# A four-layer block kernel on one core: weights of an integer feed-forward rounded by another engine, and its matrix products issued in another order

## The chip, the core and the metric

The kernel runs on one core of one Trainium2 chip. The time is in device microseconds (us) of one execution; lower is better. The engines are PE (TensorE; PEld is its weight load), DVE (VectorE), ACT (ScalarE), POOL (GpSimd) and SP (SyncE, which here only issues DMAs). Each works through its own instructions in their order and waits for others by semaphores.

## What is computed

x has 32 rows of 128 tokens by 256 features: 4096 tokens in 32 tiles of 128. Four layers follow each other, each an attention-like block and a feed-forward block, both on a layer norm and with a residual. The change touches layer 1 alone:

```python
x = x + _L1_xcond_ref(_layernorm(x, axis=-1), ctx_1024, ctx_1024, condB_tau[:, None], fside_BxS2_0, ...)
x = x + _L1_ffn_ref(_layernorm(x, axis=-1), L1_ffn_w_gate, L1_ffn_w_up, L1_ffn_w_down)

def _weight_quant(w):
    scale = 1.0 / jnp.clip(jnp.mean(jnp.abs(w)), 1e-05)
    return jnp.clip(jnp.round(w * scale), -1.0, 1.0) / scale
def _act_quant(x):
    scale = 127.0 / jnp.clip(jnp.max(jnp.abs(x), axis=-1, keepdims=True), 1e-05)
    return jnp.clip(jnp.round(x * scale), -128.0, 127.0) / scale
```

The feed-forward has three weights of 256 by 1024 (gate, up, down). Each is made of the integers -1, 0 and 1 times one scale, and the activations ahead of every product are rounded to integers with a scale per token: y = down(silu(gate(x)) * up(x)).

## The kernel before, in words

The layers are stages, each with its own blocks of instructions for the engines, one behind the other: a stage starts when all engines have ended the one before. X, the residual stream of all tiles, and MV, its row means and variances, stay in SBUF throughout.

**The attention of layer 1** (`attention`, L152) runs over 8 groups `g` of 4 tiles `u`; t = 4g + u. In tile t PE issues the output rows of tile t-2 (`output_rows`, L472), the scores of tile t+1, four turns of the probabilities (`turn_probs`, L447), and the weighting by values (`weighted_values`, L461 and L464), whose start waits for DVE's division of the tile before. Between these, except in the last group, it puts the work for the next group into the bank `ps_m`: keys in the first tile of the group, x columns in the second, queries in the third, values in the fourth. ACT (`group` from L282 on) follows in that order: the copy of the output rows (`outputs`, L280), `exps` (L273) with PE's turns, what was put into `ps_m`, and in the first tile of a group four norms of the next group's tiles (L249). DVE (L592 on) issues per tile the division of tile t-1 (`divide`, L579 and L583), the softmax of tile t+1 (L568, L573), and the row statistics of tile t-2 (`row_stats`, L136 and L138), which wait for X. POOL (`group` from L364 on) adds the rows of tile t-2 to X (`rows`, L358 and L362).

**The weights** (`BitWeights`, L632). Their loads are issued at the attention's start. In group 5 ACT sums their absolute values, one weight per tile (`magnitudes`, L664). In tile 28 PE adds these over the partitions (`totals`, L670, into `ps_m`) and DVE makes the scales from them (`scales`, L676 and L679); PE waits for that (`mean_link`) in tile 29 before it writes `ps_m` again. In tiles 29, 30 and 31 POOL rounds one weight each (`rounded`, L681), behind the rows of that tile: three passes over 128x2048 numbers, each waiting for the one before:

```python
pool.tensor_scalar(r, r, self.wscale[:, n:n + 1], ROUND, ALU.mult, ALU.add)
pool.tensor_scalar(r, r, ROUND, 1.0, ALU.subtract, ALU.min)
pool.tensor_scalar(self.wb[self.names[n]][:, :], r, -1.0, None, ALU.max)
```

ROUND is 12582912.0: what is added to it is rounded to an integer. The rows of tiles 30 and 31 come last.

**The feed-forward** (`bit_ffn`, L1318) runs over the 32 tiles. For a tile, ACT makes the norm (L1372) into one of two buffers `xn`. DVE finds the largest magnitude, makes the factor and rounds (L1479, L1483, L1486). PE turns the rows into columns (L1426). ACT takes them out as bf16 into `xqT` (L1377), which has one buffer. PE multiplies with gate and up (`gates_and_ups`, L1436) into four banks, two each; it claims each bank when ACT or DVE has emptied it. ACT applies silu to the gates (L1384), and DVE multiplies by the ups into h (L1528) and finds h's largest magnitude (L1479) and its factor (L1483). ACT rounds h (`h_rounded`, L1389), PE turns it (`h_columns`, L1446), ACT takes the columns out (L1395), and PE multiplies with down (`sums`, L1454). DVE adds the result to X and makes the row statistics (`finish`, L1511 to L1517). The order in which each engine takes the tiles is written out by hand:

```python
# ACT, tile t
gates(t + 1); h_rounded(t); norm(t + 3); h_columns(t); x_columns(t + 2)
# PE, tile t
gates_and_ups(t + 1); h_columns(t); x_columns(t + 2); sums(t)
```

DVE's tile t is h(t), the maximum of x of tile t+2, the maximum of h(t), the factors, the rounding of x of tile t+2, the dequantizing factors, and `finish(t-1)`.

## Time and profile before

| | |
|---|---|
| median of 3 runs (lowest, highest) | 3458.16 us (3453.02, 3458.41) |
| the profiled execution's own time | 3459.26 us |
| its span | 3457.5 us |
| mean granted TensorE clock over the span | 0.959 of full speed |
| PE busy | 3138.2 us (91%) |
| DVE busy | 2359.8 us (68%) |
| ACT busy | 1109.2 us (32%) |
| POOL busy | 983.6 us (28%) |
| layer 1's attention | 892.0 to 1246.5 us of the span |
| layer 1's feed-forward | 1246.5 to 1436.6 us of the span |

The shares are means over all stages with different limits and say little about the two that the change touches; those are read by their own stretches and timelines. A timeline row has the start in us from the span's start, the duration, the engine, the line, the operation with its tiles and shapes, and how many of the same kind are merged; in brackets stands how long the engine was idle before it and whose work ended that. The duration of a merged row runs from its first start to its last end. Durations of instructions that follow each other on one engine can overlap a little, so spacings are taken from starts.

### The profile page before, as it was taken

The page shows a single profiled execution, that of the slowest core. Times are in us where ns is not written, and L with a number is a line of the kernel's source. Part 1 is how long each engine was busy: PE and PEld are TensorE (multiplying, and loading weights), DVE is VectorE, ACT ScalarE, POOL GpSimd, SP SyncE. Part 2 cuts the span into 40 slices and gives each one's busy share as a digit, 9 for nine tenths or more (in the row PEclk, how much of TensorE's full clock was granted, in tenths as well). Part 3 has the DMA queues.
Part 4 walks back from the last instruction along what each step waited for, and adds up shares of the span by engine and source line. Part 5 has one row for each costly group of instructions (what it writes and reads, how often), then busy time and mean ns, then how long its engine had stood idle before and what let it go on. Part 6 is the DMA issues. An engine that isn't in the chain of part 4 may idle for free. (4 is left out here: it accounts for less than half of the span.)

```text
span 3457.5 us, 67521 instructions
## 1 busy us (share of the span) xinstructions
PE 3138.2 (91%) x27670; PEld 2384.3 (69%) x27670; DVE 2359.8 (68%) x6222; ACT 1109.2 (32%) x1989; POOL 983.6 (28%) x1010
## 2 busy tenths in 40 slices
PE   5999999899599947777899999999999987999999
PEld 4776766566377724466688888888888875777444
DVE  5777355100477758654788888888888883778666
ACT  3444211122245548643322222222222212454100
POOL 2342000233234440000244344354354352342000
PEclk9999999999799979988899999999999998999999
DMA  3100220243410000112000000000000002100000
GB/s 125 39 26 2 71 70 19 58 117 81 127 35 30 2 10 1 55 49 92 31 1 2 1 1 2 1 1 2 1 2 1 1 1 76 38 26 2 13 19 19
DMA packets 81169, 108.24 MB, mean 31 GB/s; under 512 B 11744, under 2 KB 62176, under 8 KB 80480
## 3 DMA queue, kind: packets, MB, share of 16 engines
q1 hardware_dynamic: 74720, 95.40, 8.5%
q0 software_dynamic: 6144, 8.52, 1.3%
q8 instruction: 222, 3.64, 0.4%
q14 instruction: 83, 0.68, 0.1%
HBM read 87.00 MB, written 16.91 MB: 30 GB/s over the span
## 5 line engine op out<-in xcount | busy, mean ns | idle before, releaser
L2069 POOL TENSOR_TENSOR pk_hisig<-pk_hihot,pk_sigs 128x512 f16<-128x512 f16 x512 | 520.4, 1044 | 668.3 <-DVE pk_hihot L2276 667.4
L2130 PE MATMUL pk_ps<-pk_nt,ew_downT 128*128 128x128 f32 x4096 | 515.5, 279 | 0.0
L2130 PEld LDWEIGHTS pk_ps<-pk_nt,ew_downT 128*128 128x128 f32 x4096 | 479.7, 192 | 15.3 <-issue 15.3
L2171 PE MATMUL pk_ps<-ew_up,pk_act_h 128*128 128x256 f32 x2048 | 450.4, 381 | 0.9 <-DVE pk_act_h L2264 0.9
L2171 PEld LDWEIGHTS pk_ps<-ew_up,pk_act_h 128*128 128x128 f32 x2048 | 388.8, 191 | 53.1 <-issue 1.0
L2077 ACT ACTIVATE pk_act_h<-pk_ps 128x512 f32<-128x512 f32 x256 | 152.9, 597 | 542.2 <-PE pk_ps L2130 542.2
L2277 DVE TENSOR_TENSOR pk_lohot<-pk_iota_h,pk_ps 128x1024 f16<-128x1024 f16 x256 | 310.6, 1213 | 0.0
L579 DVE RECIPROCAL a_rden<-a_ps_o 128x256 f32<-128x256 f32 x96 | 168.3, 1753 | 159.4 <-PE a_ps_o L464 159.4
L568 DVE TENSOR_REDUCE a_mx<-a_ps_s 128x8 f32<-128x1024 f32 x192 | 226.0, 1219 | 54.8 <-PE a_ps_s L438 54.5
L273 ACT ACTIVATE a_pT<-a_ps_t 128x512 f32<-128x512 f32 x384 | 208.9, 599 | 144.2 <-PE a_ps_t L447 144.0
L2450 PE MATMUL mo_ps<-mw_we,mo_xnT 128*128 128x512 f32 x512 | 225.6, 599 | 0.0
L573 DVE TENSOR_TENSOR a_probs<-a_ps_s,a_mx 128x1024 f32<-128x1024 f32 x192 | 225.2, 1214 | 0.0
L447 PE MATMUL a_ps_t<-ident,a_probs 128*128 128x128 f32 x1536 | 209.5, 279 | 4.1 <-ACT a_pT L273 4.1
L2264 DVE TENSOR_TENSOR pk_act_h<-pk_act_h,pk_ps 128x512 f32<-128x512 f32 x256 | 174.8, 683 | 43.4 <-PE pk_ps L2158 40.2
L447 PEld LDWEIGHTS a_ps_t<-ident,a_probs 128*128 128x128 f32 x1536 | 171.2, 142 | 47.4 <-issue 28.9
L362 POOL TENSOR_TENSOR X<-a_y,a_tmp 128x256 f32<-128x256 f32 x96 | 69.8, 727 | 468.9 <-ACT a_y L280 467.2
L2158 PE MATMUL pk_ps<-pk_hisig,pk_lohot 128*128 128x64 f16 x4096 | 163.8, 194 | 23.8 <-DVE pk_act_h L2264 14.4
L2450 PEld LDWEIGHTS mo_ps<-mw_we,mo_xnT 128*128 128x128 f32 x512 | 97.2, 192 | 116.9 <-issue 116.9
L2158 PEld LDWEIGHTS pk_ps<-pk_hisig,pk_lohot 128*128 128x128 f16 x4096 | 154.7, 99 | 30.2 <-DVE pk_act_h L2264 18.5
L461 PE MATMUL a_ps_o<-a_pT,a_v 128*32 128x128 f32 x3072 | 159.6, 280 | 6.8 <-DVE a_oT L583 6.8
L2276 DVE TENSOR_TENSOR pk_hihot<-pk_iota_h,pk_ps 128x256 f16<-128x256 f16 x256 | 105.1, 411 | 79.3 <-ACT pk_sigs L2097 79.3
L1301 DVE TENSOR_TENSOR ro_tmp<-ro_ps,ro_b 128x256 f32<-128x256 f32 x32 | 13.6, 424 | 212.0 <-PE ro_ps L1272 212.0
(353 smaller groups left out, 5395.4 us busy)
## 6 DMA issues: line engine op xcount, KB each, us to landing
ro_w<-in_L_W SPq DMA_DIRECT2D x16, 1024.0 KB, 7.1
a_ctx_t<-in_ctxT SPq DMA_DIRECT2D x24, 512.0 KB, 3.8
a_tau<-in_tau SPq DMA_DIRECT2D x24, 256.0 KB, 4.1
a_delta<-in_delta SPq DMA_DIRECT2D x24, 256.0 KB, 4.4
X<-in_x SPq DMA_DIRECT2D x4, 1024.0 KB, 9.4
row_dram<-sh_row SPq DMA_DIRECT2D x8, 512.0 KB, 3.0
sum_dram<-sh_new SPq DMA_DIRECT2D x8, 512.0 KB, 2.9
X<-sum_dram SPq DMA_DIRECT2D x4, 1024.0 KB, 9.5
```

The lines of the kernel that those rows point to most:

```text
L273: act.activation(pT[:, 4 * j:4 * j + 4, :], ps_t[j % 2][:, :].rearrange("p (h n) -> p h n", h=4), ACT.Exp).then_inc(t_taken, 1)
L447: ins = pe.transpose(ps_t[j % 2][:, c * P:(c + 1) * P], probs[:, parity, j, c, :], ident[:, :])
L568: dve.tensor_reduce(maxima[n], halves[n], AX_X, ALU.max).then_inc(max_ready, 1)
L573: dve.tensor_tensor(probs[:, parity, 2 * n:2 * n + 2, :, :].rearrange("p c r n -> p r c n"), halves[n], mx[:, 8 * n:8 * n + 8].rearrange(" ...
L579: dve.reciprocal(rden[:, :], ps_o[:, D:2 * D]).then_inc(den_ready, 1)
L2069: ins = pool.tensor_tensor(hisig[:, buf, n, :, :, :], hi, sig2.broadcast_to([P, TP, 2, ECH]), ALU.mult)
L2130: ins = pe.matmul(hid.bank(f"h{c}")[:, j * P:(j + 1) * P], downT[:, k, e * P:(e + 1) * P], nt[:, s, k, :], start=(k == 0), stop=(k == KC - 1))
L2158: ins = pe.matmul(wts.bank(f"w{b}")[:, j * 2 * ECH:(j + 1) * 2 * ECH], lohot[:, buf, j, :], hisig[:, buf, n, j, :, :].rearrange("p r c -> ...
L2171: ins = pe.matmul(tail.bank("y")[:, 0:D], act_h[:, s, c, :], up[:, c, :], start=(c == 0), stop=(c == ECH - 1))
L2264: wts.take(dve.tensor_tensor(hv, hv, wts.bank(f"w{b}")[:, :].rearrange("p (j c) -> p c j", c=ECH), ALU.mult), f"w{b}")
L2277: ins = dve.tensor_tensor(lohot[:, buf, :, :], *against(0, P))
L2450: ins = pe.matmul(main.bank(f"e{q}_{u}")[:, :], xnT[:, s, k, u * P:(u + 1) * P], we[:, k, 2 * q:2 * q + 2, :].rearrange("p e n -> p (e n)" ...
```

## The change

Four things, all in layer 1:

- The absolute sums move from group 5 to group 3, and totals and scales from tile 28 to tile 17 (`TOTALS_AT`). PE now issues the totals ahead of that tile's turns and waits for the scales behind two of them; DVE makes the scales ahead of the softmax.
- POOL no longer rounds. ACT does, in 24 pieces of 128x512, two at the end of each of the tiles 18 to 29: for each weight four pieces with scale and ROUND, then four that subtract ROUND and write bf16. DVE limits each weight to -1 and 1 in one pass over 128x2048 bf16, at the end of its tiles 23, 27 and 31, and PE waits for the three (`clipped`) at the start of the feed-forward.
- In the feed-forward `xqT` has two buffers. PE takes `gates_and_ups` two tiles ahead and puts it between `h_columns(t)` and `sums(t)`; `x_columns`, three ahead, comes last.
- ACT takes the x columns out ahead of the norm instead of behind the h columns.

```diff
@@ -307,8 +307,11 @@
                         queries(g + 1, 1 - s, 1, m)
                     if more and u == 3:
                         values(g + 1, 1 - s, 1, m)
-                    if integers and g == GROUPS - 3 and u < 3:
+                    if integers and g == 3 and u < 3:
                         integers.magnitudes(act, u)
+                    if integers and 0 <= t - ROUND_FROM < 12:
+                        integers.rounded(act, 2 * (t - ROUND_FROM))
+                        integers.rounded(act, 2 * (t - ROUND_FROM) + 1)
...
@@ -372,8 +375,6 @@
                         keys(g + 1, 1 - s, 0)
                         split(g + 1, 1 - s)
                         keys(g + 1, 1 - s, 1)
-                    if integers and not more and u > 0:
...
@@ -496,15 +497,18 @@
                             pe.wait_ge(xt_taken, g * 2 + 4)
                         else:
                             pe.wait_ge(q_taken, g * KC + 2 * KC)
-                        if integers and not more and u == 1:
-                            pe.wait_ge(integers.mean_link, 1)
                         output_rows(t - 2, u % 2)
                     if u < G - 1:
                         scores(g, s, u + 1)
                     elif more:
                         scores(g + 1, 1 - s, 0)
+                    if integers and t == TOTALS_AT:
+                        m_after_y(t)
+                        integers.totals(pe, ps_m[:, D:D + 3])
                     turn_probs(t, u % 2, 0)
                     turn_probs(t, u % 2, 1)
+                    if integers and t == TOTALS_AT:
+                        pe.wait_ge(integers.mean_link, 1)
                     if more:
...
-                    if integers and not more and u == 0:
-                        m_after_y(t)
-                        integers.totals(pe, ps_m[:, D:D + 3])
...
@@ -594,12 +595,14 @@
                     t = g * G + u
                     if not at_start(t, 1):
                         divide(t - 1, (u + 1) % 2)
+                    if integers and t == TOTALS_AT:
+                        integers.scales(dve, ps_m[:, D:D + 3])
                     if not (is_last(g) and u == G - 1):
                         softmax(t + 1, (u + 1) % 2)
                     if not at_start(t, 2):
                         row_stats(t - 2)
-                    if integers and is_last(g) and u == 0:
-                        integers.scales(dve, ps_m[:, D:D + 3])
+                    if integers and t >= ROUND_FROM + 5 and (t - ROUND_FROM - 5) % 4 == 0:
+                        integers.limited(dve, (t - ROUND_FROM - 5) // 4)
...
 INNER = 1024
 ROUND = 12582912.0
+TOTALS_AT = 4 * G + 1
+ROUND_FROM = TOTALS_AT + 1
...
+        self.shift = sb("shift", [P, 2])
...
-        self.mean_link, self.scales_ready, self.round_link = (
-            keep["semaphore"]("bq_mean_link"), keep["semaphore"]("bq_scales_ready"), keep["semaphore"]("bq_round_link"))
+        self.mean_link, self.scales_ready = keep["semaphore"]("bq_mean_link"), keep["semaphore"]("bq_scales_ready")
+        self.shifted, self.whole, self.clipped = (
+            keep["semaphore"]("bq_shifted"), keep["semaphore"]("bq_whole"), keep["semaphore"]("bq_clipped"))
...
     def constants(self, pool):
         pool.memset(self.ones[:, :], 1.0).then_inc(self.consts, 1)
         pool.memset(self.wmean[:, :], 0.0).then_inc(self.consts, 1)
+        pool.memset(self.shift[:, 0:1], ROUND).then_inc(self.consts, 1)
+        pool.memset(self.shift[:, 1:2], -ROUND).then_inc(self.consts, 1)
...
-    def rounded(self, pool, n):
-        r, at = self.raw[n][:, :], 3 * n
-        pool.wait_ge(self.scales_ready, 1)
-        pool.tensor_scalar(r, r, self.wscale[:, n:n + 1], ROUND, ALU.mult, ALU.add).then_inc(self.round_link, 1)
-        pool.wait_ge(self.round_link, at + 1)
-        pool.tensor_scalar(r, r, ROUND, 1.0, ALU.subtract, ALU.min).then_inc(self.round_link, 1)
-        pool.wait_ge(self.round_link, at + 2)
-        pool.tensor_scalar(self.wb[self.names[n]][:, :], r, -1.0, None, ALU.max).then_inc(self.round_link, 1)
+    def rounded(self, act, i):
+        n, q = i // 8, i % 4
+        at = slice(q * 512, (q + 1) * 512)
+        r = self.raw[n][:, at]
+        if i % 8 < 4:
+            act.wait_ge(self.scales_ready, 1)
+            act.activation(r, r, ACT.Identity, scale=self.wscale[:, n:n + 1], bias=self.shift[:, 0:1]).then_inc(
+                self.shifted, 1)
+        else:
+            act.wait_ge(self.shifted, 4 * n + q + 1)
+            act.activation(self.wb[self.names[n]][:, at], r, ACT.Identity, bias=self.shift[:, 1:2]).then_inc(
+                self.whole, 1)
+
+    def limited(self, dve, n):
+        dve.wait_ge(self.whole, 4 * n + 4)
+        b = self.wb[self.names[n]][:, :]
+        dve.tensor_scalar(b, b, 1.0, -1.0, ALU.min, ALU.max).then_inc(self.clipped, 1)
...
-        shift = sb("shift", [P, 2])
+        shift = integers.shift
...
-        xqT = sb("xqT", [P, KC, P], BF16)
+        xqT = sb("xqT", [P, 2, KC, P], BF16)
...
-        @block.gpsimd
-        def _(pool):
-            pool.memset(shift[:, 0:1], ROUND).then_inc(consts, 1)
-            pool.memset(shift[:, 1:2], -ROUND).then_inc(consts, 1)
...
             def x_columns(t):
                 xt.wait_full(act, t, "xt")
-                xt.take(act.activation(xqT[:, :, :], xt.bank("xt")[:, 0:D].rearrange("p (k n) -> p k n", k=KC),
+                xt.take(act.activation(xqT[:, t % 2, :, :], xt.bank("xt")[:, 0:D].rearrange("p (k n) -> p k n", k=KC),
                                        ACT.Identity, bias=shift[:, 1:2]), "xt")
...
-            act.wait_ge(consts, 2)
...
@@ -1408,11 +1420,11 @@
                 if t + 1 < TILES:
                     gates(t + 1)
                 h_rounded(t)
+                if t + 2 < TILES:
+                    x_columns(t + 2)
                 if t + 3 < TILES:
                     norm(t + 3)
                 h_columns(t)
-                if t + 2 < TILES:
-                    x_columns(t + 2)
...
                         gu.claim(pe, t, f"{a}{n}")
                         for k in range(KC):
-                            ins = pe.matmul(gu.bank(f"{a}{n}")[:, :], xqT[:, k, :], wt[:, k, n * 512:(n + 1) * 512],
+                            ins = pe.matmul(gu.bank(f"{a}{n}")[:, :], xqT[:, t % 2, k, :], wt[:, k, n * 512:(n + 1) * 512],
...
-            x_columns(0)
-            gates_and_ups(0)
-            x_columns(1)
+            pe.wait_ge(integers.clipped, 3)
+            for t in range(2):
+                x_columns(t)
+                gates_and_ups(t)
+            x_columns(2)
             for t in range(TILES):
-                if t + 1 < TILES:
-                    gates_and_ups(t + 1)
                 h_columns(t)
                 if t + 2 < TILES:
-                    x_columns(t + 2)
+                    gates_and_ups(t + 2)
                 sums(t)
+                if t + 3 < TILES:
+                    x_columns(t + 3)
```

## Rows read from the trace of the kernel before

**Rows 1.** By stretch: busy us (instructions) of PE, PEld, DVE, ACT, POOL; granted clock; DMA; GB/s.

```profile
1207.00:1246.50 39.50, 10.17 (x91) 7.17 (x89) 6.92 (x13) 3.34 (x8) 37.90 (x16) 0.63 0.00 0
...
1260.00:1420.00 160.00, 119.04 (x742) 71.42 (x742) 133.93 (x311) 128.02 (x200) 0.00 (x0) 0.99 0.00 1
```

**Rows 2.** Timeline of the attention's end; start, duration, engine, line, and idle time before.

```profile
1205.01 2.34 DVE L573 TENSOR_TENSOR a_probs<-a_ps_s,a_mx 128x1024 f32<-128x1024 f32 x2
...
1211.93 0.43 DVE L136 BATCH_NORM_STATS2 a_bst<-X 128x6 f32<-128x256 f32 x1 [4.58 <-POOL X L362]
...
1212.49 1.73 DVE L579 RECIPROCAL a_rden<-a_ps_o 128x256 f32<-128x256 f32 x1
...
1214.80 0.65 PE L461 MATMUL a_ps_o<-a_pT,a_v 128*32 128x128 f32 x8 [4.98 <-DVE a_oT L583]
...
1244.81 0.72 POOL L362 TENSOR_TENSOR X<-a_y,a_tmp 128x256 f32<-128x256 f32 x1
...
1246.49 1.28 ACT L1398 ACT_TABLE_LOAD   x1 [13.05 <-PEq L154]
```

**Rows 3.** Timeline, PE in tile 30: first weighting, and the output rows behind the last.

```profile
1204.47 0.42 PE L461 MATMUL a_ps_o<-a_pT,a_v 128*32 128x128 f32 x8
...
1206.35 1.13 PE L472 MATMUL a_ps_m<-a_wo,a_oT 128*128 128x256 f32 x4
```

**Rows 4.** Timeline, ACT: behind a group's four norms, and at the end of a queries tile.

```profile
1047.39 1.09 ACT L273 ACTIVATE a_pT<-a_ps_t 128x512 f32<-128x512 f32 x2 [0.96 <-PE a_ps_t L447]
...
1063.38 0.39 ACT L280 ACTIVATE a_y<-a_ps_m 128x256 f32<-128x256 f32 x1 [1.22 <-PE a_ps_m L472]
1065.19 1.08 ACT L273 ACTIVATE a_pT<-a_ps_t 128x512 f32<-128x512 f32 x2 [1.42 <-PE a_ps_t L447]
```

**Rows 5.** Timeline of one steady tile of the feed-forward, in order of start.

```profile
1331.68 1.27 ACT L1384 ACTIVATE bf_gt<-bf_ps,bf_dq 128x512 f32<-128x512 f32 x2 [0.83 <-PE bf_ps L1436]
...
1332.83 1.24 ACT L1389 ACTIVATE bf_hr<-bf_h,bf_shift,bf_asc 128x1024 f32<-128x1024 f32 x1
1333.96 0.59 ACT L1372 ACTIVATE bf_xn<-X,bf_nmr,bf_rstd 128x256 f32<-128x256 f32 x1
...
1334.12 1.09 PE L1446 MATMUL bf_ps<-ident,bf_hr 128*128 128x128 f32 x8 [1.25 <-ACT bf_hr L1389]
1334.66 0.42 DVE L1479 TENSOR_REDUCE bf_amx<-bf_xn 128x1 f32<-128x256 f32 x1 [0.71 <-ACT bf_xn L1372]
1334.82 1.27 ACT L1395 ACTIVATE bf_hqT<-bf_ps,bf_shift 128x512 bf16<-128x512 f32 x2 [0.26 <-PE bf_ps L1446]
...
1335.65 1.10 PE L1454 MATMUL bf_ps<-bq_down,bf_hqT 128*128 128x256 bf16 x8 [0.21 <-ACT bf_hqT L1395]
1335.97 0.47 ACT L1377 ACTIVATE bf_xqT<-bf_ps,bf_shift 128x256 bf16<-128x256 f32 x1
...
1336.44 0.17 DVE L1483 RECIPROCAL bf_asc<-bf_amx 128x2 f32<-128x2 f32 x1
...
1336.59 1.03 PE L1436 MATMUL bf_ps<-bq_gate,bf_xqT 128*128 128x512 bf16 x4
...
1336.98 0.48 DVE L1511 SCALAR_TENSOR_TENSOR X<-bf_ps,bf_dq,X 128x256 f32<-128x256 f32 x1
...
1337.28 1.27 ACT L1384 ACTIVATE bf_gt<-bf_ps,bf_dq 128x512 f32<-128x512 f32 x2 [0.83 <-PE bf_ps L1436]
1337.45 1.03 PE L1436 MATMUL bf_ps<-bq_up,bf_xqT 128*128 128x512 bf16 x4
...
1338.14 1.41 DVE L1528 SCALAR_TENSOR_TENSOR bf_h<-bf_ps,bf_dq,bf_gt 128x512 f32<-128x512 f32 x2
```

**Rows 6.** Groups by line and shape: the nearest rows for the new passes.

```profile
L1389 ACT ACTIVATE bf_hr<-bf_h,bf_shift,bf_asc 128x1024 f32<-128x1024 f32 x28 | 34.6, 1237 | 0.0
...
L1806 DVE TENSOR_SCALAR wa_low<-wa_inside 128x512 f32<-128x512 f32 x8 | 3.4, 427 | 0.3
...
L1086 DVE TENSOR_TENSOR sh_lohot<-sh_iota_b,sh_lo 128x2048 bf16<-128x2048 bf16 x16 | 35.9, 2287 | 7.3 <-PE sh_ps L906 7.0
```

More of the change, by code:

```diff
@@ L374, in group @@
                         keys(g + 1, 1 - s, 1)
-                    if integers and not more and u > 0:
-                        integers.rounded(pool, u - 1)
             if integers:
@@ L667, in totals @@
     def totals(self, pe, dst):
-        pe.wait_ge(self.consts, 2)
+        pe.wait_ge(self.consts, 4)
         pe.wait_ge(self.sums_ready, 3)
@@ L673, in scales @@
     def scales(self, dve, src):
-        dve.wait_ge(self.consts, 2)
+        dve.wait_ge(self.consts, 4)
         dve.wait_ge(self.summed, 1)
@@ L1353, in bit_ffn @@
         ys = Ring(f"{tag}_ys", sem, banks[7:8], ["y"])
-        consts, rstd_sq, setup = sem("consts"), sem("rstd_sq"), sem("setup")
+        rstd_sq, setup = sem("rstd_sq"), sem("setup")
         nmr_ready = sem("nmr_ready")
```

## The prediction

> **What bounds the kernel now.** The change touches two neighbouring stages, so I read the table of stretches for them first, then the timeline at their border, then the timeline of one steady tile. In the table the attention's end is a hole: from 1207.0 to 1246.5 us PE works 10.17 us and DVE 6.92 us, while POOL is busy 37.90 of 39.5 us [rows 1]. The timeline says what POOL does there. The last softmax is through at 1205.01 + 2.34 = 1207.35 us, but the next row statistics on DVE start only at 1211.93, after 4.58 us of waiting for an X that POOL adds, and behind them in DVE's order stands the division that PE needs for its last tile: PE resumes at 1214.80 [rows 2]. POOL is late because each weight's three rounding passes stand between two tiles' rows. This happens twice more, and the stage ends at 1246.49. POOL's rounding is thus the end of the attention's critical path.
>
> The feed-forward has no busy engine at its limit: in 160 us PE has 119.04, DVE 133.93, ACT 128.02 [rows 1]. One tile takes 5.60 us: ACT's `gates` starts at 1331.68 and again at 1337.28 [rows 5]. The order on ACT is the ring that sets it: gates, `h_rounded`, norm, h columns, x columns, and then 0.83 us of waiting, because PE can multiply the next gates only once those x columns exist. Another 0.26 us goes before the h columns, for PE's transposes. DVE waits 0.71 us for the norm, once per tile [rows 5]; the rest of its tile, 5.60 - 0.71 = 4.89 us, is work and its own hand-offs.
>
> **The attention's end, part by part.** *Rounding leaves POOL.* Without it X of the late tiles is there early, and DVE's order alone counts. From the softmax's end at 1207.35: row statistics and division up to PE's last weighting take 1214.80 - 1211.93 = 2.87 us, so PE starts at 1210.25. That weighting takes 1206.35 - 1204.47 = 1.88 us at the upper clock [rows 3]; 1212.15. Division to PE took 1214.80 - 1212.49 = 2.31 us [rows 2]; 1214.5. The last output rows take 1.13 us [rows 3], ACT's copy 0.39 [rows 4], and with two hand-offs (estimate 0.2) POOL's last add starts at 1216.2. From that add to the next stage it was 1246.49 - 1244.81 = 1.68 us [rows 2]. New end 1217.9, a gain of 28.6 us.
>
> *Rounding comes to ACT*, 24 pieces of 128x512, two per tile in tiles 18 to 29. No row shows such a piece. A 128x1024 pass with scale and bias takes 1237 ns [rows 6], so a piece costs between half of that and all of it; I take 0.75 us (two 128x512 gate activations, with a scale alone, take 1.27 us [rows 5]), 1.5 us per tile. Cover: ACT waits 1.22 us before the y copy and 1.42 us more before the next `exps` at the end of a tile with queries [rows 4]; there nothing shows. In the first tile of a group four norms fill that place and 0.96 us is left [rows 4]: tiles 20 and 24 run over by about 0.3 us each, 0.5 in sum, with a bound of 1.5 x 2 = 3 us. If a piece cost its upper bound of 1.24 us, 2.5 us would meet 2.64 us of waits in the other tiles, still covered. The absolute sums move from group 5 to group 3, the same work in an equal place: 0. The weights' loads are issued at the attention's start, twelve tiles ahead of the first sum, so that its wait finds them there.
>
> *Totals, scales and PE's wait for `mean_link`* move to tile 17. One small product moves with the same cost on PE. Behind the wait stand PE's second pair of turns and the next group's columns, but two of PE's turns are put ahead of it, and DVE has two instructions on three columns to do, of the size of its 0.17 us reciprocal [rows 5]; 0, bounds 0 and 1 us. Tile 28 loses the same work, which I don't count.
>
> *The clamp on DVE*, three times 128x2048 bf16. Lower rows: 128x512 f32 in 427 ns; at most four times that, 1.7 us; upper: a two-input bf16 pass of 128x2048 in 2287 ns [rows 6]. I take 1.7. Two fall in tiles where DVE waits for PE. The third stands in tile 31 ahead of the last division: DVE is free at about 1210.7 and the division is due at 1212.2, so 1.5 us are hidden: 0.2 us on the path, bounds 0 and 0.8. The Trainium skill ("VectorE: DVE Perf Modes", the perf-mode tier table) gives 693 ns for a one-source bf16 pass of 2048 elements; by that the term would be 0 instead of 0.2, and no row here shows such a pass. A rule there speaks against the change: "ScalarE: Activation LUTs" (rules for kernel authors) puts plain multiplications, additions and limits on VectorE, not ScalarE. In rows, 24 passes of 427 ns on DVE would put four of them, 1.7 us, into tiles 28 and 29, where DVE no longer waits for PE; the rule would make this sum 1.7 us worse.
>
> Attention: -28.6 + 0.5 + 0.2 = **-27.9 us**.
>
> **The feed-forward, part by part.** With two buffers of x columns and PE's `gates_and_ups(t+2)` ahead of `sums(t)`, the gates of tile t+1 are ready when ACT comes to them: the wait of 0.83 goes. `x_columns` ahead of the norm fills the 0.26 as well: from `h_rounded`'s end PE needed 1334.82 - 1333.96 = 0.86 us, and columns and norm now take 0.47 + 0.59. ACT's tile becomes 1.15 + 1.13 + 0.47 + 0.59 + 1.15 = 4.5 us [rows 5]. What is late next? I check each ring against DVE's 4.89:
> - ACT, norm, DVE, ACT: `h_rounded` to norm is now 1.13 + 0.48; norm to DVE's maximum 1334.66 - 1333.96 = 0.70; maximum to reciprocal 1336.44 - 1334.66 = 1.78; the reciprocal and its hand-off 0.2. Sum 4.3. The norm moved back by 0.48 is covered by 0.6.
> - PE for DVE's `finish(t-1)`: from `h_rounded` 1334.12 - 1332.83 = 1.29 to its transposes, at most 1.0 for these (their duration is 1.09, overlapping the next), gates and ups 2 x (1337.45 - 1336.59) = 1.72, sums 1336.59 - 1335.65 = 0.94; 4.95 plus 0.15 for the last to drain. `finish` is due at 4.89 - 0.2 + (1336.98 - 1336.44) = 5.23. Slack 0.15: the thinnest place.
> - PE's ups wait for DVE to empty the two banks of h(t+1): DVE is through (1338.14 - 1336.44) + 1.41 = 3.1 us after its reciprocal, and PE comes to the first of them after 0.2 + 1.29 + 1.0 + 0.86 = 3.35. Free by 0.25 us.
> - PE's own work, 119.04 / 160 x 5.6 = 4.2 us [rows 1], is under 4.89.
>
> So DVE's order bounds it: 4.89 us, 0.71 less. There are 31 steps from tile to tile; I take the first two as the ramp: 29 x 0.71 = 20.6 us. (The last two lack DVE's work for x, before as after; not counted.) In the first tiles nothing is won: `h_rounded(0)` starts as before, and the norm behind the columns costs the first ring about 0.5, which the second gives back. The clock's dip there stays (PE's granted clock was low when it came back after its hole, and the stage's mean is 0.99 [rows 1]). Bounds: 0.71 whole, and, if the 0.15 of slack is not there, 0.3 to 0.4 less per tile, 10 us. Feed-forward: **-20.6 us**.
>
> **Sum.** -27.9 - 20.6 = -48.5 us. The profiled execution took 3459.26 us (span 3457.5); it becomes 3410.8. The median of the runs, 3458.16, stands 1.1 lower: **3409.6 us**. A measurement of this kernel can tell about 0.2%, 7 us, from no change.
>
> **The rivals.**
> A, a new ring in the feed-forward: `sums(t)` behind eight more matmuls makes DVE's `finish` wait. For: slack of 0.15 us only, on modelled PE ends. Against: each duration is a row. Period 5.1 to 5.3 instead of 4.89: 6 to 12 us given back, about 3419. Chance 0.17.
> B, the period does not move at all, the 0.83 us reappearing elsewhere on the ring (the bank claims): only the attention's part is left, 3458.2 - 27.9 = 3430. Against: 0.25 us or more of room on each ring. Chance 0.06.
> C, the pieces are not covered on ACT: 1.5 us in each of twelve tiles on PE's path, 18 us: 3428. Against: the waits of 1.22 and 1.42 us. Chance 0.05.
> D, slower than before: PE's clock. It fell to the lower level in holes of this border, where the eight-matmul weighting took longer (0.65 for 0.42 us [rows 2, 3]). If PE stayed at 1.2 GHz through the feed-forward, its 4.0 us of bound work per tile become 7.9, PE bounds, and 32 x (7.9 - 4.89) = 96 us come on top: 3506. It decides once some 16 of the 32 tiles run so. For: the stage starts after a hole still. Against: before, PE was idle 1.4 us per tile and the grant was 0.99; after, it idles less. The Trainium skill ("TensorE: Matmul & The Clock Gate", part 1) says throttled is the default state and activity releases it; by that rule a shorter, denser tile keeps the upper level, and the trace agrees with 0.99. Chance 0.02.
>
> **How the numbers follow.** My case, 0.70, gives 3409.6, with bounds of its own: below, 0.7 less for the terms taken at cost, 1.3 if the clock's dip at the start goes, and the runs' own 5 us downward; above, 3 for the pieces, 1 for the wait, 0.6 for the clamp, 3 for half of rival A's size. Range 3402 to 3424 takes in A. Left out are B, C and D and the ends, under 0.2. Faster by over 0.2% means below 3451: my case, A, B and C, 0.97 with what is unforeseen taken off; the same 0.01; slower 0.02.
>
> **What would show it.** In the profile after: the attention's hole between last softmax and next stage about 11 us instead of 39; no POOL rounding; ACT pieces of 0.7 to 0.8 us in twelve tiles without a longer PE group; DVE's wait for the norm gone, ACT's idle time ahead of `gates` now a wait for DVE's factors ahead of `h_rounded`; period 4.89. Wrong it would be if `finish` waited for PE each tile, if groups 4 to 6 grew by over 1 us, or if the granted clock in the feed-forward fell below 0.9.

## The result, and the profile after

| | before | after |
|---|---|---|
| median (lowest, highest) | 3457.35 us (3453.02, 3458.41), 4 runs | 3403.94 us (3402.39, 3405.29), 4 runs |
| ratio of the times, 95% interval | | 0.9846 (0.9834 to 0.9859) |
| span of the profiled execution | 3457.5 us | 3400.7 us |
| PE, DVE, ACT, POOL busy | 3138.2, 2359.8, 1109.2, 983.6 us | 3130.2, 2355.8, 1120.8, 939.7 us |
| attention, from its first output copy (L280) to the next stage | 306.00 us | 277.45 us |
| feed-forward | 190.15 us | 165.30 us |
| its period per tile | 5.60 us | 4.72 us |

The change saves 53.4 us; the sum of the forecast was 48.5. By the two profiles, 28.6 lie in the attention and 24.8 in the feed-forward. The stages ahead of both have the same code in all kernels here, and still the attention's first output copy starts anywhere from 933.93 us (e1) to 941.36 us (e5). So I measure the attention from the copy of its first output rows (940.49 us before, 937.68 after) to the table load that opens the feed-forward (1246.49, 1215.13), and the feed-forward from there to the table load of the stage behind (1436.64, 1380.43).

The timeline of the attention's end, kernel after; it answers to [rows 2]:

```profile
1202.21 2.35 DVE L574 TENSOR_TENSOR a_probs<-a_ps_s,a_mx 128x1024 f32<-128x1024 f32 x2
...
1207.34 0.43 PE L462 MATMUL a_ps_o<-a_pT,a_v 128*32 128x128 f32 x8 [0.91 <-DVE a_oT L584]
...
1207.75 0.66 DVE L706 TENSOR_SCALAR bq_down<-bq_down 128x2048 bf16<-128x2048 bf16 x1
1209.36 1.76 DVE L580 RECIPROCAL a_rden<-a_ps_o 128x256 f32<-128x256 f32 x1 [0.95 <-PE a_ps_o L465]
...
1213.45 0.72 POOL L365 TENSOR_TENSOR X<-a_y,a_tmp 128x256 f32<-128x256 f32 x1 [1.13 <-ACT a_y L280]
...
1215.13 1.28 ACT L1411 ACT_TABLE_LOAD   x1 [1.82 <-PEq L154]
```

From the last softmax's end (1202.21 + 2.35 = 1204.56) to the next stage it is now 10.57 us; before it was 1246.49 - 1207.35 = 39.14. POOL, which was busy through the hole, now waits for ACT's copies. The last clamp (L706) takes 0.66 us and ends at 1208.41, before PE's weighting lets the last division start at 1209.36: DVE waited 0.95 us behind it, so the clamp isn't on the path.

ACT's timeline in tiles 18 to 20 shows the pieces in their place, against [rows 4]:

```profile
1097.76 1.51 ACT L696 ACTIVATE bw_gate<-bw_gate,bq_shift,bq_wscale 128x512 f32<-128x512 f32 x2
...
1100.89 1.08 ACT L273 ACTIVATE a_pT<-a_ps_t 128x512 f32<-128x512 f32 x2 [1.35 <-PE a_ps_t L448]
...
1117.29 2.06 ACT L249 ACTIVATE a_xn<-X,a_nmr,a_rstd 128x256 f32<-128x256 f32 x4
1119.25 1.32 ACT L700 ACTIVATE bq_gate<-bw_gate,bq_shift 128x512 bf16<-128x512 f32 x2
1120.48 0.36 ACT L280 ACTIVATE a_y<-a_ps_m 128x256 f32<-128x256 f32 x1
1120.74 1.06 ACT L273 ACTIVATE a_pT<-a_ps_t 128x512 f32<-128x512 f32 x2
```

Two pieces with a scale take 1.51 us, two with a bias alone 1.32. They eat the wait of 1.22 us ahead of the y copy; that of 1.42 ahead of `exps` stays at 1.35. Only behind the four norms, in tile 20 (and again in 24), is no wait left.

One steady tile of the feed-forward, in order of start; it answers to [rows 5]:

```profile
1303.12 0.17 DVE L1497 RECIPROCAL bf_asc<-bf_amx 128x2 f32<-128x2 f32 x1
1303.32 1.24 ACT L1402 ACTIVATE bf_hr<-bf_h,bq_shift,bf_asc 128x1024 f32<-128x1024 f32 x1 [0.32 <-DVE bf_asc L1497]
...
1303.66 0.48 DVE L1525 SCALAR_TENSOR_TENSOR X<-bf_ps,bf_dq,X 128x256 f32<-128x256 f32 x1
...
1304.46 0.45 ACT L1390 ACTIVATE bf_xqT<-bf_ps,bq_shift 128x256 bf16<-128x256 f32 x1
...
1304.61 1.09 PE L1458 MATMUL bf_ps<-ident,bf_hr 128*128 128x128 f32 x8 [0.38 <-ACT bf_hr L1402]
1304.63 0.18 DVE L1531 BATCH_NORM_AGGREGATE MV<-bf_bst 128x2 f32<-128x6 f32 x1
1304.74 1.41 DVE L1542 SCALAR_TENSOR_TENSOR bf_h<-bf_ps,bf_dq,bf_gt 128x512 f32<-128x512 f32 x2
1304.82 0.59 ACT L1385 ACTIVATE bf_xn<-X,bf_nmr,bf_rstd 128x256 f32<-128x256 f32 x1
1305.31 1.26 ACT L1408 ACTIVATE bf_hqT<-bf_ps,bq_shift 128x512 bf16<-128x512 f32 x2
...
1306.07 0.41 DVE L1493 TENSOR_REDUCE bf_amx<-bf_xn 128x1 f32<-128x256 f32 x1
...
1306.46 1.27 ACT L1397 ACTIVATE bf_gt<-bf_ps,bf_dq 128x512 f32<-128x512 f32 x2
...
1307.27 1.04 PE L1466 MATMUL bf_ps<-bq_down,bf_hqT 128*128 128x256 bf16 x8
...
1307.83 0.17 DVE L1497 RECIPROCAL bf_asc<-bf_amx 128x2 f32<-128x2 f32 x1
...
1308.38 0.48 DVE L1525 SCALAR_TENSOR_TENSOR X<-bf_ps,bf_dq,X 128x256 f32<-128x256 f32 x1
...
1312.56 0.17 DVE L1497 RECIPROCAL bf_asc<-bf_amx 128x2 f32<-128x2 f32 x1
```

ACT's wait of 0.83 us for the gate products is gone, and so is DVE's wait of 0.71 for the norm. ACT now waits 0.32 us ahead of `h_rounded`, for DVE's factor. The list of waits from 1240 to 1370 us says that this holds in every tile (us in total, times, longest):

```profile
PE bf_ps L1458 <- ACT bf_hr L1402: 10.4, 27, 0.4
ACT bf_hr L1402 <- DVE bf_asc L1497: 8.7, 28, 0.3
...
DVE X L1525 <- PE bf_ps L1466: 0.3, 1, 0.3
```

DVE waits once in 28 tiles, so its own order sets the period; the experiments below find a second ring of nearly the same length. The stretches show the ends of the stage (columns as in [rows 1]):

```profile
1215.13:1235.00 19.87, 12.54 (x60) 6.60 (x61) 12.25 (x34) 15.16 (x24) 0.00 (x0) 0.76 0.14 42
1235.00:1370.00 135.00, 116.95 (x742) 73.67 (x740) 129.68 (x314) 125.25 (x199) 0.00 (x0) 1.00 0.00 1
1370.00:1380.43 10.43, 5.76 (x32) 3.92 (x32) 5.98 (x15) 4.43 (x7) 0.00 (x0) 0.84 0.00 0
```

### The profile page after: what moved, and what is told of

Read it like the earlier page. It is cut to its first block and busy times, and to the rows that moved or that the text cites. A ratio compares the mean times of both kernels' runs of the same rounds, so it can differ in the third digit from the quotient of the medians.

```text
span 3400.7 us, 67538 instructions
## 1 busy us (share of the span) xinstructions
PE 3130.2 (92%) x27670; PEld 2384.9 (70%) x27670; DVE 2355.8 (69%) x6225; ACT 1120.8 (33%) x2013; POOL 939.7 (28%) x1001
## 5 line engine op out<-in xcount | busy, mean ns | idle before, releaser
L574 DVE TENSOR_TENSOR a_probs<-a_ps_s,a_mx 128x1024 f32<-128x1024 f32 x192 | 225.2, 1215 | 0.0
L2172 PEld LDWEIGHTS pk_ps<-pk_hisig,pk_lohot 128*128 128x128 f16 x4096 | 154.7, 99 | 30.2 <-DVE pk_act_h L2278 18.5
```

The lines of the kernel that those rows point to most:

```text
L574: dve.tensor_tensor(probs[:, parity, 2 * n:2 * n + 2, :, :].rearrange("p c r n -> p r c n"), halves[n], mx[:, 8 * n:8 * n + 8].rearrange(" ...
L2172: ins = pe.matmul(wts.bank(f"w{b}")[:, j * 2 * ECH:(j + 1) * 2 * ECH], lohot[:, buf, j, :], hisig[:, buf, n, j, :, :].rearrange("p r c -> ...
```

## The experiments

Two questions: do the two halves add, and what sets each of them now? In all kernels the stages are cut as above. One row per kernel, in us. The time is a median where an interval stands, else that of one execution, which can be a few us off; each ratio is to the runs of before made beside that kernel (medians 3457.35 beside the changed kernel, 3459.24 beside e1 and e2, 3455.08 beside e11 and e12). The stages are each read from one profile; the attention's length repeats within 0.04 us (277.42 to 277.46) in the eight kernels that share its code.

| kernel | attention | feed-forward | period | time, ratio to before |
|---|---|---|---|---|
| before | 306.00 | 190.15 | 5.60 | 3457.35 |
| after | 277.45 | 165.30 | 4.72 | 3403.94, 0.9846 (0.9834 to 0.9859) |
| e1, feed-forward alone | 305.67 | 163.88 | 4.72 | 3429.03, 0.9919 (0.9903 to 0.9936) |
| e2, attention alone | 277.43 | 189.21 | 5.60 | 3426.68, 0.9911 (0.9894 to 0.9927) |
| e3, after, ACT's order of before | 277.43 | 191.36 | 5.53 | 3429.37 |
| e4, after, PE's order of before | 277.46 | 240.16 | 7.10 | 3478.54 |
| e5, after, POOL rounds the weights early | 277.13 | 165.58 | 4.72 | 3405.28 |
| e6, after, POOL rounds x | 277.43 | 164.75 | 4.71 | 3404.87 |
| e8, after, pieces doubled | 280.21 | 165.45 | 4.72 | 3405.33 |
| e9, after, `finish` later | 277.42 | 163.28 | 4.70 | 3403.24 |
| e10, e6 and e9 together | 277.46 | 157.64 | 4.47 | 3391.88 |
| e12, e10 timed | 277.46 | 157.65 | 4.47 | 3394.29, 0.9824 (0.9811 to 0.9838) |
| e11, e10 with e5 | 277.18 | 156.67 | 4.47 | 3396.42, 0.9828 (0.9814 to 0.9841) |

**The two halves apart.** e1 keeps the change's feed-forward and takes the attention of before, POOL's rounding at its end included; e2 is the reverse. Their edits are the change's own hunks.

> The feed-forward of the changed kernel (two column buffers, gates two tiles ahead on PE, x columns ahead of the norm on ACT) behind the attention of before, where POOL rounds in tiles 29 to 31. If the two parts are independent, the stage takes 165 us instead of 190 and the time is 24.9 us under before, about 3432.5. Rival: the shorter stage owes part of its time to the shorter hole in front of it (PE's clock at its start); then the stage would take 168 us or more here. The attention stays at 306 us from its tile 0 output copy to its end.

> The attention of the changed kernel (ACT rounds in tiles 18 to 29, sums and totals early) with the feed-forward's orders of before on both engines. Independent parts: 28.5 us under before, about 3429, with the feed-forward at 190 us and 5.60 us per tile. Rival: the parts interact, and the two single gains sum to less or more than the 53.4 us by over 2 us.

Measured: e1 shortens the feed-forward by 26.3 us and the attention by 0.3; e2 shortens the attention by 28.6 and the feed-forward by 0.9. Together that is 56.1 us, and the change has 53.4: the sum is off by 2.7, more than the 2 us of e2's rival. The steady periods are 4.72 and 5.60 in either company. What differs is mostly the ends of the feed-forward, where PE's granted clock is low for some us:

- Behind the long hole (e1) the stage takes 163.9 us, behind the short one 165.3. e1's first `h_rounded` comes 0.5 us sooner after the stage's start, and its last is 0.96 us nearer to the end; the granted clock of its last 10 us is 1.00, not 0.84.
- e2's 0.9 comes from the start: before has 6.95 us from the first `h_rounded` to the second, with a granted clock of 0.65 from 1262 to 1266 us; e2, with the same orders, has 5.60 there, but starts 0.4 later.

So the halves are independent but for these ends. The medians can't tell more: e1 is 30.2 us under before and e2 32.6, where 24.9 and 28.5 were expected, with 95% intervals that reach some 6 us to either side of each. The surplus of the feed-forward over the forecast is there in e1 as well, so it doesn't hang on the attention's new end.

**Which half of the new order does it?** e3 puts ACT's x columns back behind the h columns, e4 gives PE its old order; both keep the two buffers.

```diff
 # e3, ACT
                 h_rounded(t)
-                if t + 2 < TILES:
-                    x_columns(t + 2)
                 if t + 3 < TILES:
                     norm(t + 3)
                 h_columns(t)
+                if t + 2 < TILES:
+                    x_columns(t + 2)
 # e4, PE
...
             for t in range(TILES):
+                if t + 1 < TILES:
+                    gates_and_ups(t + 1)
                 h_columns(t)
                 if t + 2 < TILES:
-                    gates_and_ups(t + 2)
+                    x_columns(t + 2)
                 sums(t)
-                if t + 3 < TILES:
-                    x_columns(t + 3)
```

> The changed kernel with ACT's x columns back at the end of its tile, behind the h columns; PE's order and two buffers stay. Theory (rings of hand-offs): x columns end 3.6 us behind the start of h_rounded, gates and ups behind them at 5.4, sums at 6.4, and DVE's finish waits for those; from finish to the factors two tiles on it is 4.2 us, so two tiles take 10.8 us: 5.4 us per tile, about 3424. Rival: two buffers and gates ahead on PE suffice, 4.7 to 4.9 us per tile, 3404 to 3409.

> The changed kernel with PE's order of before (gates one tile ahead, sums last); ACT's x columns stay ahead of the norm. Theory: ACT now waits for PE's x transposes, which stand behind the h transposes, then comes the norm, then the h columns, then sums and only then the next gates: 7.2 us per tile, 1.6 more than before, about 3478, slower than before. Rival: the order on ACT saves its 0.26 us or nothing by itself, 5.3 to 5.6 us per tile, 3420 to 3429.

Measured: 5.53 us per tile with the columns last, 7.10 with the gates one tile ahead. e3 gives nearly the period of before, where 5.4 was expected; e4, as expected, is slower than before, by 19 us in the whole kernel (one execution of 3478.54 against 3459.24 for before). The waits of e3, 1260 to 1350 us:

```profile
PE bf_ps L1448 <- ACT bf_xqT L1390: 23.9, 17, 1.5
ACT bf_gt L1397 <- PE bf_ps L1448: 12.9, 17, 0.8
DVE X L1525 <- PE bf_ps L1466: 11.4, 16, 0.7
```

PE may run two tiles ahead, but the x columns that it needs come last on ACT: PE stands for them up to 1.5 us, and ACT's own gates, next in its order, wait 0.8 us for PE. It is ACT's old ring unchanged: gates 1.16, `h_rounded` 1.13, norm 0.85 with a wait of 0.26, h columns 1.16, x columns 0.47 and the wait of 0.76 make 5.53. That ring binds, and not the one that I had expected. The second buffer and PE's order give next to nothing without ACT's: 0.07 us per tile. e4's waits, same stretch:

```profile
DVE bf_amx L1492 <- ACT bf_xn L1385: 27.3, 12, 2.3
...
PE bf_ps L1466 <- ACT bf_hqT L1408: 20.6, 12, 1.7
ACT bf_xqT L1390 <- PE bf_ps L1438: 18.2, 13, 1.4
ACT bf_gt L1397 <- PE bf_ps L1448: 16.4, 12, 2.2
```

Here ACT asks for the x columns right behind `h_rounded`, and PE makes them only behind `h_columns`, which themselves wait for `h_rounded`. ACT stands 1.4 us, everything behind it on ACT is late by that, DVE waits 2.3 us for the norm, and the gates come late as well. On top of that, four of its later steps take 8.3 to 8.4 us instead of 7.11, and the granted clock is low in them: 0.53 from 1271 to 1274 us in the first. In these two kernels each order is good only with the other.

**Is it ScalarE, or the earlier place, that freed the attention's end?** e5 leaves the rounding on POOL, with the same three passes per weight, but one pass in each of nine tiles from 18 to 29.

```diff
+POOL_PASSES = (18, 19, 21, 22, 23, 25, 26, 27, 29)
...
 # POOL, end of tile t
+                    if integers and t in POOL_PASSES:
+                        integers.rounded(pool, POOL_PASSES.index(t))
...
 # ACT and DVE
-                        integers.rounded(act, 2 * (t - ROUND_FROM))
-                        integers.rounded(act, 2 * (t - ROUND_FROM) + 1)
...
-                        integers.limited(dve, (t - ROUND_FROM - 5) // 4)
```

> The changed kernel, but POOL rounds as before, its nine passes of 2.0, 7.1 and 5.4 us spread one by one over tiles 18 to 29, none in the first tile of a group; sums and totals early as in the changed kernel, no pieces on ACT, no clamp on DVE. Theory (the place in time counts, not the engine): POOL's idle time per such tile is over 8 us, so nothing is late, and from the first output copy to the stage's end it takes 277.4 us or up to 1 us less (ACT's lateness in tiles 18, 20, 22, 24 goes), against 306.0 before. Rival: POOL is too slow wherever it rounds, rows or keys come late, 285 us or more.

Measured: 277.13 us, 0.3 less than with ACT's pieces. POOL's timeline in tiles 18 and 19:

```profile
1093.54 1.97 POOL L693 TENSOR_SCALAR bw_gate<-bw_gate,bq_wscale 128x2048 f32<-128x2048 f32 x1
...
1103.26 0.72 POOL L362 TENSOR_TENSOR X<-a_y,a_tmp 128x256 f32<-128x256 f32 x1 [7.05 <-ACT a_y L280]
1103.95 7.11 POOL L695 TENSOR_SCALAR bw_gate<-bw_gate 128x2048 f32<-128x2048 f32 x1
...
1113.11 0.73 POOL L362 TENSOR_TENSOR X<-a_y,a_tmp 128x256 f32<-128x256 f32 x1 [1.34 <-ACT a_y L280]
```

Even a pass of 7.11 us fits between two tiles' rows, and POOL waits another 1.34 us behind it. The whole gain of the attention's half comes from rounding earlier, which the earlier scales allow; ACT's pieces with DVE's clamps cost 0.3 us more than POOL's passes in the same tiles.

**How far are the pieces from costing something?** e8 doubles them.

```diff
                         integers.rounded(act, 2 * (t - ROUND_FROM) + 1)
+                        integers.extra(act, 2 * (t - ROUND_FROM))
+                        integers.extra(act, 2 * (t - ROUND_FROM) + 1)
...
```

> The changed kernel with ACT's work for the weights made twice as large: two more passes of 128x512 (scale 1, with a bias, f32) per tile in tiles 18 to 29, into a tile that nobody reads; the result is the same. A piece with a bias alone takes 709 ns in the changed kernel, so a tile gets some 1.35 us more. Theory (the pieces are free because ACT waits 1.35 to 1.43 us for PE's turns even with them): ten of the twelve tiles still hide them, the first tiles of groups 5 and 6 (tiles 20 and 24), whose place is filled by four norms, run over by up to 1.35 us each; attention from the first output copy to its end 279 to 281 us instead of 277.4. Rival (the pieces lie on the path by now): twelve times 1.35 us, 294 us. The feed-forward keeps its 165.3 us.

Measured: 280.21 us, 2.8 more for twelve extra pairs of 1.47 us. ACT's timeline in tiles 18 to 20:

```profile
1097.53 1.51 ACT L699 ACTIVATE bw_gate<-bw_gate,bq_shift,bq_wscale 128x512 f32<-128x512 f32 x2
1098.94 1.47 ACT L708 ACTIVATE bq_sized<-bw_down,bq_shift 128x512 f32<-128x512 f32 x2
...
1100.66 1.08 ACT L273 ACTIVATE a_pT<-a_ps_t 128x512 f32<-128x512 f32 x2
...
1110.52 1.08 ACT L273 ACTIVATE a_pT<-a_ps_t 128x512 f32<-128x512 f32 x2 [0.24 <-PE a_ps_t L450]
...
1121.88 1.07 ACT L273 ACTIVATE a_pT<-a_ps_t 128x512 f32<-128x512 f32 x2
```

The second pair fills what was left: the wait of 1.35 us behind the pieces of tile 18 is 0, that of 1.42 behind those of tile 19 is 0.24. Counted from each kernel's first output copy (937.46 and 937.68 us), these `exps` start at 163.20, 173.06 and 184.42 us; in the changed kernel at 163.21, 173.06 and 183.06. Behind tile 20, the first of its group, they are 1.36 us late, behind the other two they are not. The total of 2.8 is about twice that, for the first tiles of groups 5 and 6. The rival's 294 us is far off. The feed-forward keeps its length (165.45).

**What bounds the feed-forward at 4.72?** Two things are close: DVE's order (4.72), and a ring over two tiles. In the rows above it runs from `h_rounded` (1303.32) over PE's transposes, gates, ups and sums to the sums' end (1307.27 + 1.04 = 1308.31, so 4.99; PE's ends are modelled), into DVE's `finish` and through its tile to the reciprocal behind that, the second after the ring's start (1312.56 - 1308.38 = 4.18), and with the 0.2 to its `h_rounded` it is 9.4 for two tiles, 4.70 each. e6 takes an instruction of 0.35 us off DVE (the next one started 0.27 behind it), e9 takes `finish` out of the ring, e10 does both.

```diff
 # e6: x of tile t rounded by POOL instead of DVE
...
+        @block.gpsimd
+        def _(pool):
+            for t in range(2, TILES):
+                pool.wait_ge(asc_ready, t - 1)
+                pool.tensor_scalar(xn[:, t % 2, :], xn[:, t % 2, :], asc[:, t % 2, 0:1], ROUND, ALU.mult,
+                                   ALU.add).then_inc(xr_ready, 1)
 # DVE
...
-                if more:
-                    x_rounded(t + 2)
...
 # e9: finish behind h of the next tile
...
+                if t >= 2:
+                    finish(t - 2)
                 dve.wait_ge(dq_ready, t + 2)
...
-                if t >= 1:
-                    finish(t - 1)
...
+            finish(TILES - 2)
```

> The changed kernel with the rounding of x in the feed-forward moved from DVE to the idle POOL. If DVE's own order alone bounds the 4.72 us per tile, it falls by the 0.27 us of that instruction to 4.45, and the stage by 8 us. Rival (my ring of hand-offs): from h_rounded to the end of the sums it is 4.99 us, from DVE's finish to the next factors 4.18, to h_rounded 0.2; two tiles then need 9.4 us, so the period stays at 4.70, and DVE now waits for PE ahead of finish by about 0.25 us per tile.

> The changed kernel with DVE's finish of a tile one step later, behind the next product h instead of ahead of it. DVE's work is the same, so if DVE bounds it, the period stays at 4.72 us, within 0.03, and the stage at 165 us. Rival: a hand-off bounds it and the period moves by over 0.05.

> Both: x rounded on POOL, and finish one step later. The ring through the sums is open now, so DVE's order bounds it again, less 0.27: 4.45 us per tile, stage 157 us, the time about 8 us under the changed kernel's. ACT's work of 4.3 us and PE's 4.2 per tile stay under it. Rival: the period stays at 4.70.

Measured: 4.71, 4.70 and 4.47 us. Each alone gives nearly nothing per tile, both together 0.25 us and 7.7 us in the stage. (e9's stage is 2.0 us shorter all the same: 0.7 by its 0.02 to 0.03 per tile, the rest in the first and last tiles.) What e6 takes from DVE comes back as a wait for the sums in every second tile:

```profile
1300.53 0.17 DVE L1504 RECIPROCAL bf_asc<-bf_amx 128x2 f32<-128x2 f32 x1
...
1301.29 0.48 DVE L1532 SCALAR_TENSOR_TENSOR X<-bf_ps,bf_dq,X 128x256 f32<-128x256 f32 x1 [0.40 <-PE bf_ps L1473]
...
1305.48 0.17 DVE L1504 RECIPROCAL bf_asc<-bf_amx 128x2 f32<-128x2 f32 x1
...
1309.95 0.17 DVE L1504 RECIPROCAL bf_asc<-bf_amx 128x2 f32<-128x2 f32 x1
```

4.95 and 4.47 us alternate, 9.42 for two tiles, the ring's 9.4. In e9 ACT still waits 0.3 us for DVE in each tile: there DVE's order bounds, at 4.70. With both gone the list of waits of e12, 1235 to 1360 us, names no wait of every tile for ACT or DVE any more, and ACT is busy 117.3 of 120 us:

```profile
ACT bf_hr L1409 <- DVE bf_asc L1504: 1.0, 3, 0.4
ACT bf_hqT L1415 <- PE bf_ps L1465: 0.4, 1, 0.4
DVE bf_h L1549 <- issue: 0.3, 1, 0.3
DVE bf_amx L1500 <- issue: 0.2, 1, 0.2
```

So e10's theory, that DVE's order alone bounds it again, isn't shown: ACT is nearly full as well, and no run takes work from one of the two at this period.

**The version that beats both.** e12 is e10's code, timed; e11 adds e5's early rounding on POOL.

> The same code as e10_both, timed: the changed kernel with x rounded by POOL and finish(t-1) moved behind h(t) of the next tile. From its profile (feed-forward 157.64 us against 165.30 in the changed kernel): 7.7 us under the changed kernel's 3403.9, about 3396.3, and 61 us under before, ratio about 0.982. If the 3391.9 of its first single execution were typical it would be 66 us under.

> e10_both with the rounding of the weights on POOL (three passes per weight, one per tile in tiles 18 to 29, as in e5_pool_early) in place of ACT's pieces and DVE's limits. Theory (the two parts are independent): attention 277.1 us as in e5, feed-forward 157.6 as in e10, period 4.47; 0.3 us under e12_both_timed, which the medians can't tell from no change. Rival (the parts touch, for instance POOL's last rounding delays the start of the feed-forward): over 1 us more in either stage.

Measured: e12 takes 3394.29 us (3392.85 to 3397.36, 5 runs) where before takes 3455.08 beside it: 60.8 us less, against 53.4 for the change, and 61 were expected. e11 takes 3396.42 (3392.69 to 3398.87); its interval covers e12's. Its stages are as the theory has them but for 1.0 us less in the feed-forward. Of that, 0.7 is two tiles of 4.84 and 4.82 us in e12, in each of which DVE stands 0.2 to 0.3 us for "issue", a wait whose cause the profile doesn't show; e11 has none. The medians stand the other way round by 2.1 us, so the two can't be told apart.

## Why the prediction was right, and where it was off

- **POOL's rounding is the end of the attention's critical path: right.** Term -28.6; the hole is 10.57 us where the working has 1217.9 - 1207.35 = 10.55 (added up without rounding in between, it gives 10.46). e2 shows the part alone, e5 shows that the place in time does it.
- **The attention's small terms: 0.7 us was charged, and the sum is nothing, but only because a term that was left out cancels them.** Counted from each kernel's first output copy, DVE's softmax (`a_probs`, L573 before, L574 after) is later than before by 1.02 us up to tile 21 (starts at 183.60 and 184.62), by 0.35 in tiles 22 to 25 (191.78, 192.13), by 0.50 in 26 to 28 (229.26, 229.76) and by 0.02 from tile 29 on (257.27, 257.29). The parts can be read off. The absolute sums cost 0.8 us wherever they stand, in group 3 now (PE's output rows start at 112.09, not 111.29) and in group 5 before, so they cancel, as forecast. Totals and scales in tile 17 leave 0.2, where 0 was taken. The pieces cost 0.14 in each of tiles 20 and 24, 0.3 where 0.5 was charged. Against that stands 0.5 that before lost in tile 28, where totals and scales stood: the work that the prediction didn't count.
- **The pieces: right in mechanism, a little too dear.** 0.75 us each was taken; the rows show 0.76 and 0.66 (half of 1.51 and 1.32). e5, which has none of them, is 0.3 us shorter, the same 0.3 as tile by tile above. e8 confirms the cover: rival C is excluded.
- **The clamp: mis-sized.** 1.7 us was taken, four times the 427 ns of a 128x512 f32 pass; it measures 0.66 us, and DVE waits another 0.95 behind it, so the term is 0 and not 0.2. The Trainium skill ("VectorE: DVE Perf Modes", the perf-mode tier table) gives 693 ns for such a pass: the trace agrees within 5%, and the page's figure was the better one. Its rule on ScalarE ("ScalarE: Activation LUTs", rules for kernel authors) wasn't tried, since no run puts the 24 passes on VectorE.
- **The feed-forward: right in mechanism, the period mis-sized.** DVE's order does bound it, with ACT waiting for the factor as foretold. But "the rest of its tile, 5.60 - 0.71 = 4.89 us, is work and its own hand-offs" was 0.17 too large. First, DVE's row of h lasts 1.41 us, but the next instruction starts 1306.07 - 1304.74 = 1.33 us after it, once it has nothing to wait for: 0.08. Before, 1.41 and the 0.71 of waiting stood one behind the other. Second, the statistics' last row led h by 1338.14 - 1337.96 = 0.18 us before and by 1304.74 - 1304.63 = 0.11 now: 0.07, probably a wait for ACT's gates too short to be listed. The rest, 0.02, is spread over the tile.
- **The feed-forward's ends: put at nothing, and they weren't.** The gain is 24.8 where 20.6 was forecast, and the starts of `h_rounded` say where. The 28 steps from the third to the last but one gain 24.7 (156.80 us before, 132.12 now). The first two gain 3.1 (6.95 and 5.59 before, 4.28 and 5.13 now), 1.35 of it the clock's dip of before that e2 doesn't have. The last step loses 1.6 (3.14, now 4.69); the kernels with PE's old order keep 3.14 there (e2, e4). The first `h_rounded` comes 0.45 later after the stage's start (12.20, now 12.65), and the last stands 0.96 further from its end (5.47, now 6.43). At both places PE's granted clock was lower than before: 0.72 against 0.93 some 8 to 12 us into the stage, and 0.84 against 1.00 in the last 10 us.
- **The range held partly by luck.** All of the miss is a gain, and 3403.94 us lies 2 us above the range's lower end. No bound of the prediction stood for a period below 4.89; what covered the 0.17 us per tile was the 5 us allowed for the scatter of the runs.
- **Rival A, `finish` waits for the sums: it did not bind, by 0.02 us.** The thinnest place was named rightly: its ring takes 4.70 us per tile, DVE's order 4.72. It binds as soon as DVE's order gets 0.27 us shorter (e6), and then at 4.71, where the rival had 5.1 to 5.3.
- **Rival B, the wait reappears elsewhere: false for the change,** but e3 shows it is what happens with PE's half alone (5.53), and e4 that the other half alone is worse than nothing (7.10).
- **Rival D, the clock: false.** The steady stretch has 1.00. The dip at the start stayed (0.76 over 20 us, 0.71 before), and one came at the end: PE's last eight transposes, after 2.07 us of waiting, took 1.97 us. The wait alone doesn't decide that: in e1 the same transposes after the same wait took 1.09, and behind waits of 1.6 us they took 1.97 in e12 and 1.09 in e11. Why the clock falls in one and not in the other stays open. After, then e1:

```profile
1375.29 1.97 PE L1458 MATMUL bf_ps<-ident,bf_hr 128*128 128x128 f32 x8 [2.07 <-ACT bf_hr L1402]
...
1399.30 1.09 PE L1445 MATMUL bf_ps<-ident,bf_hr 128*128 128x128 f32 x8 [2.07 <-ACT bf_hr L1389]
```

## What to carry to other kernels

Work that only has to be ready for the next stage is best put where its engine waits in mid-stage; it is the earlier place that pays, and here ACT and POOL did it alike, to 0.3 us. When two engines pass tiles to each other in orders written by hand, change both orders together and follow each ring around: here one half alone gave next to nothing and the other cost 50 us in the stage. Where a trim of the busiest engine gives nothing, look for a second ring of the same length, over two tiles if need be, and cut both.

## What the runs showed of the hardware

- On DVE an instruction that waits for nothing can start some 0.08 us before the recorded end of the one ahead of it (h to maximum: 1.33 us from start to start, 1.41 us long). A period worked out from durations and waits comes out too long by that at each wait that goes. The Trainium skill ("VectorE: DVE Perf Modes", "The DRAIN you can't avoid") has the next instruction start only when the pipeline of the one ahead is empty, and adds that one which is not held starts earlier; the trace agrees with the latter in direction.
- At one size, 128x2048 f32, POOL's passes differ by operation: multiply and add 1.97 us, subtract and minimum 7.11 us (e5's rows above), and the maximum with bf16 output 5.4 us.
- PE's granted clock can differ at the same place in two kernels with the same wait ahead of it: 1.97 and 1.09 us for eight transposes behind 2.07 us of waiting (the changed kernel and e1).
- DVE's limit to two constants over 128x2048 bf16 in place took 0.66 us, against 2.29 us for the two-input pass of [rows 6].
